# Scoring the first pair's vector-turned key groups last, and turning two more key groups on VectorE in the later pairs

## The reference: what is computed

```python
x = x + xattn(layernorm(x), ctx, ctx, Wq, bq, Wk, bk, Wv, bv)   # softmax(q k^T * scale) v, 1601 keys
x = x + attn(layernorm(x), Wq, Wk, Wv, gq, gk, Wo, bo, ln_w, ln_b)
x = x + ffn(layernorm(x), gate_w, w_gate, w_up, w_down)         # one of 8 experts for each row
```

## Time and profile before

| | before |
|---|---|
| median of 3 runs | 381.05 us (380.95 to 381.32) |
| the profiled execution: its own time | 382.74 us |
| its span, first to last instruction | 380.6 us |
| PE busy | 343.1 us (90%) |
| DVE busy | 161.4 us (42%) |
| ACT busy | 93.9 us (25%) |
| pair 1, from its first score to that of pair 2 | 95.92 to 155.97 us |
| pair 3, from its first score on | 216.50 us |

### The profile page before, as it was taken

One profiled execution on the slowest core, in us unless ns is written; L12 is line 12 of the kernel. 1 busy time (PEld: TensorE's weight loads), 2 busy tenths in 40 slices (PEclk: granted clock), 3 DMA queues, 4 the chain that ended last, 5 costly groups with the idle time before them and its releaser, 6 DMA issues.

```text
span 380.6 us, 5836 instructions
## 1 busy us (share of the span) xinstructions
PE 343.1 (90%) x2154; PEld 214.9 (56%) x2154; DVE 161.4 (42%) x357; ACT 93.9 (25%) x215; POOL 81.9 (22%) x87
## 2 busy tenths in 40 slices
PE   1999189999999989999998999999889988799993
PEld 1777056853546644455653455643436778788781
DVE  4126018423253755280757254332463644255322
ACT  1232012135113481111663112242313300000000
POOL 4000007332024200223400210332023302512122
PEclk9999759879999999999999999999999999899998
DMA  7999999928999205999301997100891142910000
GB/s 265 268 185 334 365 386 219 183 61 297 384 197 184 51 0 193 370 293 187 62 0 53 344 372 296 43 0 2 339 420 67 50 175 102 342 68 19 30 25 26
DMA packets 48613, 69.05 MB, mean 181 GB/s; under 512 B 2598, under 2 KB 27206, under 8 KB 47568
## 3 DMA queue, kind: packets, MB, share of 16 engines
q1 hardware_dynamic: 46592, 62.94, 59.0%
q0 software_dynamic: 2000, 5.83, 4.1%
HBM read 65.61 MB, written 4.19 MB: 183 GB/s over the span
## 4 chain that ended last, share of the span: by engine, by line
PE 66%; SPq 10%; issue 6%; DMA 6%; DVE 4%; ACT 4%; POOL 3%; DVEq 0%; ACTq 0%; POOLq 0%
PE ST L1071 12%; PE A L975 11%; PE SC L1046 9%; PE A L1254 8%; PE TR L970 7%; SPq L298 6%; DMA AW_sb<-awk 4%; PE TR L975 4%; PE SC L1236 3%; PE A L970 2%; PE A L1017 2%; SPq L285 2%; SPq L288 1%; SPq L309 1%; PE SC L1211 1%
## 5 line engine op out<-in xcount | busy, mean ns | idle before, releaser
L1071 PE MATMUL ST<-CTX_sb,PR_sb 128*64 128x512 f32 (+1 forms) x208 | 47.7, 599 | 2.2 <-ACT PR_sb L276 2.2
L970 PE MATMUL TR<-ident_sb,CTX_sb 128*128 128x128 f32 (+1 forms) x224 | 31.0, 282 | 11.0 <-DMA CTX_sb<-ctx 10.1
L970 PEld LDWEIGHTS TR<-ident_sb,CTX_sb 128*128 128x128 f32 (+1 forms) x224 | 24.9, 147 | 22.2 <-DMA CTX_sb<-ctx 10.9
L688 DVE STREAM_TRANSPOSE CT_sb<-FF_sb 128x1024 f32<-128x1024 f32 x24 | 28.3, 1218 | 14.6 <-DMA FF_sb<-ctx 13.9
L269 DVE COPY CT_sb<-TR 128x512 f32<-128x512 f32 (+1 forms) x28 | 18.3, 654 | 30.1 <-PE TR L970 26.2
L1071 PEld LDWEIGHTS ST<-CTX_sb,PR_sb 128*64 128x64 f32 (+1 forms) x208 | 14.1, 136 | 25.4 <-issue 22.2
L269 ACT COPY CT_sb<-TR 128x512 f32<-128x512 f32 (+1 forms) x28 | 15.5, 553 | 48.4 <-PE TR L970 48.3
L1046 PE MATMUL SC<-CT_sb,qcurP_sb 128*64 128x256 f32 x192 | 26.9, 404 | 0.0
L1046 PE MATMUL SC<-CT_sb,qcur_sb 128*64 128x256 f32 x192 | 25.3, 389 | 0.0
L975 PE MATMUL A<-AW_sb,normT_sb 128*128 128x512 f32 x48 | 22.0, 600 | 0.0
L423 POOL TENSOR_TENSOR rn_sb<-ss_sb,nhalf_sb 128x16 f32<-128x16 f32 x4 | 11.6, 2907 | 39.7 <-DVE ss_sb L762 39.7
(11 more groups left out here) (243 smaller groups left out, 525.7 us busy)
## 6 DMA issues: line engine op xcount, KB each, us to landing
CTX_sb<-ctx SPq DMA_DIRECT2D x24, 1024.0 KB, 9.3
FF_sb<-ctx SPq DMA_DIRECT2D x32, 256.0 KB, 8.8
FF_sb<-ctx SPq DMA_DIRECT2D x32, 128.0 KB, 5.9
CTX_sb<-wgu SPq DMA_DIRECT2D x4, 1024.0 KB, 9.1
CTX_sb<-wdn SPq DMA_DIRECT2D x5, 512.0 KB, 11.1
FF_sb<-wgu SPq DMA_DIRECT2D x2, 1024.0 KB, 6.2
rows<-XR_sb SPq DMA_DIRECT2D x3, 512.0 KB, 10.2
CTX_sb<-ctx SPq DMA_DIRECT2D x8, 130.0 KB
```

The costliest lines, as they stand in the source:

```text
L688: v.transpose(ctxT[:, grp % 2, k, :, :].rearrange("p c (b r) -> p b c r", r=Q), split[:, k, n * BLOCKS:(n + 1) * BLOCKS, :].rearrange("p b ...
L970: last = t_.transpose(bank[:, c * w:c * w + n], rows[:, c * P:(c + 1) * P], ident[0:n, 0:n])
L1071: last = t_.matmul(ST[q, :], probs[0:w, t, q], ctxb[0:w, k, t, :], start=(t == 0), stop=(t == KT - 1))
```

## The change

The order of groups becomes an object for each kind of pair. Pair 0 (`FIRST`) scores groups 2, 4, 5, 6 and then the split groups 0, 1, 3; the later pairs (`NEXT`) keep the order 0 to 6 and have five split groups, 0, 1, 3, 4, 5, in three slots of `FF_sb`. Groups 4 and 5 of a pair are loaded into the slots of groups 0 and 1 once these are turned (`last_split`), and groups 0 and 1 of the next pair go there once group 5 is turned (`next_split`). ACT's `next_queries` in the loop is taken out from in front of the exponentials and comes in two halves behind them. In pair 0 the context is loaded ahead of the split groups, except chunk 0, and PE's first turned tile no longer waits for chunk 0.

```diff
-SPLIT_GROUPS = (0, 1, 3)
+SLOT_OF = {0: 0, 1: 1, 3: 2, 4: 0, 5: 1}
+SPLIT_PARTS = ((0, 1), (3,), (4, 5))
+EARLY = 2
...
+FIRST = Order((2, 4, 5, 6, 0, 1, 3), (0, 1, 3))
+NEXT = Order((0, 1, 2, 3, 4, 5, 6), (0, 1, 3, 4, 5))
...
+            def next_split(p):
+
+                sp.wait_ge(s["keysT_made"], split_turned(p, order_of(p).split.index(3) + 1))
+                settle(sp)
+                load_split(p + 1, 1)
+                sp.wait_ge(s["keysT_made"], split_turned(p, len(order_of(p).split)))
+                settle(sp)
+                load_split(p + 1, 0)
...
-            load_split(0)
-            load_pair(0, (1, 2, 3, 0))
+            load_pair(0, (1, 2, 3))
+            load_split(0, 0)
+            load_split(0, 1)
+            load_pair(0, (0,))
             load_weight(wv, "wv", "wv_in")
...
-            load_split(1)
+            next_split(0)
...
+            def last_split(p):
+
+                sp.wait_ge(s["keysT_made"], split_turned(p, 2))
+                settle(sp)
+                load_split(p, 2)
+
             with sp.Fori(1, PAIRS - 1) as p:
+                last_split(p)
                 load_x(p)
-                load_split(p + 1)
+                next_split(p)
                 load_pair(p + 1)
                 store_rows(p - 1)
+            last_split(PAIRS - 1)
...
-                if not is_last(p):
-                    next_queries(p + 1)
                 exponentials(p)
                 for step in by_max:
                     attention(p - 1, step)
                 move_numerators(act, a.copy, p, 0)
                 for c in range(NCH):
+                    if c in (0, 3) and not is_last(p):
+                        next_queries(p + 1, NEXT.at[NEXT.split[-1]] + 1, (0, 1) if c == 0 else (2, 3))
...
-                        if t == min(i for i in TURNED_TILES if i >= lo):
+                        if lo <= t < hi and t == min(i for i in o.tiles if i >= lo):
                             pe.wait_ge(s_ctx[k][c], 16 * p + 16)
```

More of the change, by code:

```diff
@@ L19, with __init__, tile, split_at @@
 BLOCKS = GT * P // Q
-SPLIT_GROUPS = (0, 1, 3)
-SPLIT_LOADS = ((0, 2), (2, 3))
-TURNED_TILES = [t for t in range(KT) if t // GT not in SPLIT_GROUPS]
+SLOT_OF = {0: 0, 1: 1, 3: 2, 4: 0, 5: 1}
+SPLIT_PARTS = ((0, 1), (3,), (4, 5))
+EARLY = 2
 CHUNKS = [(0, 4), (4, 8), (8, FULL), (FULL, KT)]
 NCH = len(CHUNKS)
+class Order:
+    def __init__(self, groups, split):
+        self.groups = groups
+        self.split = [g for g in groups if g in split]
+        self.at = {g: i for i, g in enumerate(groups)}
+        self.tiles = [t for g in groups if g not in split for t in range(g * GT, min(g * GT + GT, KT))]
+        last = sorted((max(self.at[t // GT] for t in range(lo, hi)), c) for c, (lo, hi) in enumerate(CHUNKS))
+        self.ready = {c: at + 1 for at, c in last}
+        self.maxima = [c for _, c in last]
+        self.max_at = {2 * at + 3: c for at, c in last if 2 * at + 3 < 2 * GROUPS}
+    def tile(self, u):
+        pos = u // GT + 1
+        t = self.groups[pos] * GT + u % GT if pos < GROUPS else KT
+        return t if t in self.tiles else None
+    def split_at(self, u):
+        pos = u // GT + 1
+        return self.groups[pos] if u % GT == 0 and pos < GROUPS and self.groups[pos] in self.split else None
+FIRST = Order((2, 4, 5, 6, 0, 1, 3), (0, 1, 3))
+NEXT = Order((0, 1, 2, 3, 4, 5, 6), (0, 1, 3, 4, 5))
 HEADS, HD = 16, 32
@@ L529, in _, with next_queries @@
                 move_qk(True, m)
-            def next_queries(p):
+            def next_queries(p, last, chunks=range(DC)):
                 act.wait_ge(s["qk_moved"], 2 * DC)
-                act.wait_ge(s["scored"], GROUPS * (p - 1) + SPLIT_GROUPS[-1] + 1)
-                for m in range(DC):
+                act.wait_ge(s["scored"], GROUPS * (p - 1) + last)
+                for m in chunks:
                     for j in range(QUADS):
@@ L619, in pair @@
                         attention(p - 1, step)
[L620 to L622 removed]
+                    move_keys(act, a.copy, p, 0, NEXT.tile(u))
                 exponentials(p)
@@ L885, in pair @@
                         attention(p - 1, step)
-                    if c < 2 and not is_last(p):
-                        turn_split(p + 1, c)
+                    if c < EARLY and not is_last(p):
+                        turn_split(p + 1, NEXT.groups[c])
             with dve.Fori(1, PAIRS - 1) as p:
@@ L1045, in score @@
                         q = slice(k * S, (k + 1) * S)
-                        last = t_.matmul(out[q, :], (qcurP if split_group else qcur)[:, c, q], ctxT[:, grp % 2, k, c, 0:n], start=(c == 0), stop=(c == DC - 1))
+                        last = t_.matmul(out[q, :], (qcurP if split_group else qcur)[:, c, q], ctxT[:, pos % 2, k, c, 0:n], start=(c == 0), stop=(c == DC - 1))
                 if half == 1:
@@ L1157, in scores @@
             def scores(p, by_scores):
-                first = isinstance(p, int) and p == 0
-                if first:
+                o = order_of(p)
+                if is_first(p):
+                    for t in o.tiles[:GT]:
+                        turn_keys(p, t)
                     bring(False, 0)
```

138 lines of the change are left out of this document (77 added, 61 removed).

## The result

The changed kernel takes 387.1 us (median of 4 runs, 386.27 to 388.13), the kernel before on the same chip 381.19; the ratio is 1.0145, with a 95% interval of 1.0103 to 1.0187. A second comparison with more runs (the last experiment) gives 385.29 against 380.93 and 1.0121 (1.0086 to 1.0156). So the change costs 4.4 to 5.9 us by the medians, where +1.2 was forecast. The sign was right, and the size was missed by a factor of four to five. The first median lies above the range of 378.2 to 386.0, that of the repeat 0.7 us inside its upper end.

A forecast was written before the change was run, and what follows sets the result against it. PE, busy 90% of the span, was taken as the bound, except in pair 0, where loads up to `awk`, then DVE, bind. Terms 4.3 - 1.2 - 1.2 - 0.7 = +1.2 us on 381.05 gave 382.3 us, range 378.2 to 386.0.

The forecast's parts named there:

- Pair 0, +4.3: Pair 0: split groups stand behind the first gate reduction in DVE's list, so bias matmuls start later; +4.3 us, between +3.7 and +10.
- The open part, the clock: Pair 0: PE idles 10 us, its clock falls, and slow scores or bias matmuls may add to the loss; most likely recovers scoring group 1.
- the working's 3.7: Pair 0: loss of 3.7 us from scores ending at 73.8 instead of 70.16, before anything for the clock.
- The first rival: Pair 0: clock stays at 1.2 GHz for third split group, bias matmuls and those behind; term +7.4, time 385.4; chance 0.15.
- the third: Pair 0 loses nothing because `awk` lands 3 us or more earlier; 4.3 less, time about 378.0; chance 0.08.
- Pairs 1 and 2, -1.2 each: Pairs 1 and 2: fewer PE turnings and earlier exponentials, partly lost waiting for groups 0 and 1; -1.2 us each, bounds 0 and -2.1.
- DVE is done with its steps q and k at 122.06, turns group 4: Pairs 1 and 2: DVE turns group 4 from 122.06 until 124.45, and PE waits 1 us for it.
- the fourth rival: Load of groups 0 and 1 is 2 us later than thought; nothing gained in pairs 1 and 2, 384.7 us; chance 0.07.
- Pair 3, -0.7: Pair 3: four turnings saved, less PE waits of 2.2 us for group 4 and 0.7 for group 5; -0.7 us, bounds 0 and -2.9.
- The second rival, the later loads in time (378.3): Pairs 1 to 3: later split loads arrive in time, pairs give 7.1 us, sum -2.8, time 378.3; chance 0.26.

The follow-up runs named there:

- the last experiment: The changed kernel itself, repeated with more runs against the kernel before: 385.29 us against 380.93, ratio 1.0121.
- e1: Changed kernel's pair 0 order alone; later pairs keep the split groups, loads and query copies of the kernel before: 384.62 us, ratio 1.0092.
- e4: Changed kernel with DVE's eight wgate reductions of pair 0 moved behind its shift, and POOL's bias copy ahead of its products: 376.35 us, ratio 0.9850.
- e9: Changed kernel with unused identity matmuls filling two PE waits, 70 in pair 0 and 20 ahead of group 4 in pair 3: 386.2 us, ratio 1.0103.
- e7: Changed kernel with the loads of groups 4 and 5 issued between context chunks 1 and 3 instead of behind all four: 382.84 us, ratio 1.0030.
- e6: Changed kernel without the loads of groups 4 and 5, their scores made from keys of groups 0 and 1: 380.91 us, ratio 0.9967.
- e10: Changed kernel with pair 0's reductions behind DVE's shift and its next-pair turnings behind both numerator copies; later pairs split only groups 0, 1, 3: 373.69 us, ratio 0.9749.
- e11: Changed kernel, pair 0's reductions and next-pair turnings later, groups 4 and 5 loaded earlier, groups 0 and 1 turned one chunk later in pairs 1, 2: 369.06 us, ratio 0.9629.

## Why the prediction came out as it did

**Pair 0, +4.3: right in its mechanism, 0.6 too high.** The first reduction started at 61.00 (60.1 in the text), the third group was turned at 71.8 (71.6), the bias matmuls started at 73.76 (73.8), and pair 1 began 3.67 us later. e1 measures it as +3.5, e4 shows the mechanism. The open part, the clock, was put at +0.6 there; e9 shows that it cost nothing, and without it the working's 3.7 is what came. The third group's 1.95 us say that the clock was back at full for it, as the text took it. The first rival (low clock through the third group) did not come, nor did the third (`awk` earlier).

**Pairs 1 and 2, -1.2 each: right in pair 2, wrong in pair 1.** Pair 2 gave -1.17 with the waits named: 1.00 for group 4, 1.17 of DVE for the load of groups 0 and 1, and h behind it. Pair 1 gave +0.4 in the first profile and 0.0 in the repeat. The first step that failed there is "DVE is done with its steps q and k at 122.06, turns group 4": it took the load of groups 4 and 5 as landed by then, 26.1 us after the pair's start, without working out when it lands. DVE got it 27.3 us after the start, and PE waited 2.13 us (1.60 in the repeat) instead of 1.

What the pair then ended with was set by the second load. Group 5 was turned 33.6 us after the start (33.1 in the repeat) where the text has 32.6, and the load of groups 0 and 1, which is issued behind it, took another 14.1 us (14.3) until DVE had it, where the text has 13.3. So h came 50.6 us after the start (50.2), where the text has 49.1 and the kernel before 50.3, and nothing was gained. That is the fourth rival, come true in pair 1 alone, with 1.5 to 1.9 us instead of its 2. The repeat shows it without the clock: there it stayed up, the weighted sum started 44.2 us after the start, 2.0 us earlier than before and within 0.2 us of the forecast, and the wait of 1.77 us for h took it all back. In the first profile the fall of the clock made the sum late (45.8), but DVE had to wait for the load even so (0.54), so the half clock can have cost pair 1 little.

**Pair 3, -0.7: the largest miss.** Its timetable held well: q came 18.2 us after the pair's start where it had been 20.3, the 2.0 earlier that the text had; the load was there after 23.7 us and not 22.7; PE waited 3.41 us in all and not 2.9. The term was still +1.72, 2.4 off. The three matmul groups behind the wait took 3.68, 1.13 and 2.17 us, where the same work takes 1.95, 0.71 and 1.95 in pairs at full clock: 2.4 us of half clock. This is the step that failed: the text weighed the clock in pair 0 alone, and counted the waits of 2.2 and 0.7 us in pair 3 at the price of the waits, with nothing for the half clock behind them. e9 gives 1.3 us of it back, or by an estimate 1.9 without its overrun of 0.57, so most of it is shown and the rest is the sum by rows. Without this miss the first median, too, would have been in the range.

**The rest of the gap.** By the parts the profiled execution has 3.66 + 0.39 - 1.17 + 1.72 = 4.6 us, the medians of the repeat differ by 4.4, and the parts' ratios say 4.1. The two spans differ by 5.4, since the ending has 0.8 more, and its length varies between executions by more than that (129.7 us behind the last column in the changed kernel, 127.6 in its repeat, 128.9 before). The first comparison's 5.9 rests on four runs of each kernel. What goes beyond the parts is scatter as far as the runs here show, and no effect of the change.

**The second rival, the later loads in time (378.3),** was a good count of what the load costs. e7 moves it up: pair 3 gains 3.5 us against the kernel before, where the text had 2.9. It did not come about in the changed kernel, because the loads of this layout move at the rate of the earlier trace rows, 171 to 187 GB/s in the stretches from 114 to 130 and from 238 to 242 here, and not at that of the context. The rule of the Trainium skill (DMA: Bandwidth & Descriptors, Specifications), that pieces of 512 bytes are enough for line rate, is again not borne out. What the sum lacked was that such a load may also share the queue with others: from 110 to 126.87 the view of stretches has 2.8 MB moved, and the load is 2.1 MB, so at least 0.7 MB of other loads came ahead of its last bytes. DVE had it 27.3 us after the start in pair 1, where more split loads were issued behind it from 120.40 on, and 23.7 us after in pair 3, where none were; 1.1 us of that is its later issue. No run tries the sharing by itself.

**Where it could have been seen.** Two rows stood in front of the reader and were used only for pair 0: the clock had fallen in a hole of 8.45 us, and the forecast itself had PE waiting 1 to 3 us in three more places. Whether the clock would fall behind so short a wait was not to be had from the kernel before, and the runs give no clean answer either. In the two profiles of the changed kernel it fell, in pairs 1 to 3, behind waits of 2.13, 3.33 and 3.41 us and not behind those up to 1.77. In the other kernels it fell behind a wait of 1.90 (e7), 1.96 (e6) and 1.98 (e10), and did not behind 1.97 and 2.23 (e4) and 2.27 (e11). With 2.4 us of half clock behind the wait in pair 3 the forecast would have been 384.7. The Trainium skill (TensorE: Matmul & The Clock Gate, Why this matters for your kernels) warns of idle gaps between bursts of matmuls; it was cited for pair 0, where the half clock cost nothing, and left out in pair 3, where it did.

## What to carry to other kernels

In-order lists turn a reordering of one engine's work into a wait on another: before moving work to the end of a stage, look up what the helping engine has ahead of it there, and for what that waits. Here the new order was worth 8.9 us of pair 0 and lost 3.7, for eight small reductions, the last of them done at 74.5, whose result PE first uses at 119.18. A load added behind others has to be given a landing time by its own layout's rate, from its issue on, and where PE waits for it, the price can be the wait and slow matmuls behind it: here 3.41 us and another 2.4.

## What was not expected of the hardware

PE's clock fell to 0.50 in 13 of the 14 profiles (all but that of e10) around the 16 matmuls that follow the 32 bias matmuls of one column each, also where PE had been busy throughout. With the filler of e9 ahead of them, the view of stretches has:

```profile
66.00:68.00 2.00, 2.00 (x19) 1.82 (x19) 2.00 (x3) 0.00 (x0) 1.10 (x1) 1.00 0.00 0
...
74.00:76.00 2.00, 2.00 (x19) 1.89 (x17) 1.84 (x3) 0.00 (x0) 0.10 (x1) 1.00 0.96 224
78.00:80.00 2.00, 2.00 (x7) 1.39 (x7) 0.37 (x2) 0.48 (x2) 0.19 (x1) 0.50 1.22 192
80.00:82.00 2.00, 2.00 (x5) 1.09 (x4) 0.00 (x0) 2.00 (x8) 0.00 (x0) 0.50 1.24 175
```

The busy column says 2.00 of 2.00 all the way, and the 16 matmuls took 7.92 us, where e10, without the fall, has 5.41:

```profile
65.23 5.41 PE L1087 MATMUL A<-AO_sb,WQK_sb 128*128 128x384 f32 x16
```

So a full busy row doesn't by itself mean that the clock is held; whether it is the single columns or something else of these instructions was not tried. The clock's falls also differ between executions of one program (in pair 1 of the changed kernel it fell in one of two profiles), which may be part of the scatter of 1 to 2 us between runs.
